# Attention over three merged key blocks: the products of blocks 1 to 3 of a group issued as one run on TensorE

## What is computed

```python
qkv = x @ Wqkv + bqkv
att = softmax(where(causal, q @ k.T * scale, -inf))     # 512 x 512 for each head
x = layernorm(x + (att @ v) @ Wout + bout)
h = silu(lin(x, w1)) * lin(x, w2)                        # 1024 hidden channels
h = gelu(lin(h, h1))
h = gelu(lin(h, h2))
x = layernorm(x + lin(h, w3))                            # lin: einsum with a weight, times a scale
```

## Time and profile before

| | us |
|---|---|
| median of 3 timed runs (2322.57 to 2328.25) | 2323.64 |
| profiled execution, its own time | 2323.13 |
| its span in the profile | 2321.4 |
| TensorE busy in it | 2208.8 (95%) |
| VectorE, ScalarE, GpSimd busy | 1278.9, 1293.6, 488.1 |
| TensorE products for `pO` (L973) | 2048 records in 209 unbroken runs: 162 of 8 and 47 of 16 |

### The profile page before, as it was taken

How to read it: one execution, slowest core, us unless ns; L and a number is a source line. 1 busy time by engine, 2 the same in 40 slices (tenths; PEclk the granted TensorE clock), 3 DMA queues, 4 the chain that set the end, 5 groups by cost and what they waited for, 6 DMA issues and landing times.

```text
span 2321.4 us, 52007 instructions
## 1 busy us (share of the span) xinstructions
PE 2208.8 (95%) x16294; PEld 1871.2 (81%) x16294; DVE 1278.9 (55%) x3961; ACT 1293.6 (56%) x2769; POOL 488.1 (21%) x896
## 2 busy tenths in 40 slices
PE   4758999999999999999999999999999999999998
PEld 2336888888888888888888888888888888888898
DVE  4564565555556556555655556565555656555433
ACT  1334566565656656565665656656565565656543
POOL 1121222122222212212221222212122221222211
PEclk7779999999999999999999999999999999999999
DMA  8642223232232323223232232323223232312000
GB/s 288 209 142 63 66 59 74 55 76 60 63 71 59 75 55 71 65 61 71 61 75 55 67 69 61 70 61 75 55 61 75 59 69 64 75 42 50 23 6 10
DMA packets 96838, 166.18 MB, mean 72 GB/s; under 512 B 21568, under 2 KB 40768, under 8 KB 96576
## 3 DMA queue, kind: packets, MB, share of 16 engines
q1 hardware_dynamic: 88736, 139.02, 25.9%
q10 hardware_dynamic: 7840, 23.86, 3.0%
HBM read 93.08 MB, written 71.83 MB: 71 GB/s over the span
## 4 chain that ended last, share of the span: by engine, by line
PE 77%; DMA 4%; issue 3%; SPq 3%; ACT 2%; DVE 2%; POOL 0%; ACTq 0%; DVEq 0%; POOLq 0%
PE ring L1055 38%; PE ring L1041 8%; PE pM L951 6%; PE pO L973 6%; PE pS L939 6%; PE ring L1068 5%; PE ring L985 4%; PE ring L1021 2%; DMA dn<-den_d 2%; DMA qk_d<-c 2%; PE ring L1005 1%; SPq L504 1%; DVE full_g L805 1%; PE ring L959 1%; ACT L698 1%
## 5 line engine op out<-in xcount | busy, mean ns | idle before, releaser
L766 DVE CUSTOM_DVE_ANT_0 pM<-pM,mask 128x512 f32<-128x512 f32 (+3 forms) x1024 | 493.4, 507 | 318.7 <-PE pM L951 262.5
L1055 PE MATMUL ring<-Xhi,H 128*128 128x256 f32 x2048 | 515.4, 291 | 6.6 <-ACT full_h L711 5.0
L1055 PE MATMUL ring<-Yhi,H 128*128 128x256 f32 x2048 | 507.4, 285 | 0.0
L1055 PE MATMUL ring<-Ylo,H 128*128 128x256 f32 x2048 | 502.8, 283 | 0.0
L1055 PE MATMUL ring<-Xlo,H 128*128 128x256 f32 x2048 | 499.3, 282 | 0.0
L1055 PEld LDWEIGHTS ring<-Xhi,H 128*128 128x128 f32 x2048 | 391.1, 191 | 18.7 <-ACT full_h L711 11.7
L1055 PEld LDWEIGHTS ring<-Ylo,H 128*128 128x128 f32 x2048 | 390.9, 191 | 3.2
L1055 PEld LDWEIGHTS ring<-Xlo,H 128*128 128x128 f32 x2048 | 392.1, 191 | 1.1
L1055 PEld LDWEIGHTS ring<-Yhi,H 128*128 128x128 f32 x2048 | 390.2, 191 | 2.6
L951 PE MATMUL pM<-Ks,Qs 128*128 128x512 f32 x992 | 297.4, 358 | 48.4 <-DMA Ks<-qk_d 31.4
L710 ACT ACTIVATE Yhi<-ring,cols 128x256 fp32r<-128x256 f32 x256 | 120.8, 472 | 285.8 <-PE ring L1055 251.2
(11 more groups left out here) (102 smaller groups left out, 3336.8 us busy)
## 6 DMA issues: line engine op xcount, KB each, us to landing
qk_d<-c SPq DMA_DIRECT2D x124, 256.0 KB, 3.4
Qs<-qk_d SPq DMA_DIRECT2D x124, 192.0 KB, 4.4
Ks<-qk_d SPq DMA_DIRECT2D x124, 192.0 KB, 4.9
qk_d<-c SPq DMA_DIRECT2D x124, 128.0 KB, 3.1
xTs<-in_xT SPq DMA_DIRECT2D x16, 512.0 KB, 4.4
raw<-in_h ACTq DMA_DIRECT2D x8, 1024.0 KB, 24.5
xz<-in_x SPq DMA_DIRECT2D x16, 512.0 KB, 6.5
Oc<-Osb SPq DMA_DIRECT2D x256, 32.0 KB
```

The lines of the kernel that those rows point to most:

```text
L766: nc.vector.tensor_tensor_reduce(pM[:, h % 2, 0:n], pM[:, h % 2, 0:n], mask[:, T - n:T], 1.0, NEG, ALU.add, ALU.max, mx[:, t, h:h + 1]).th ...
L1055: mm = nc.tensor.matmul(to, w, x_part, start=(k == 0 and m == 0), stop=(k == KB - 1 and m == 1))
```

## The change

`pv` has only two steps for a group now: `pv:0:g:0` (block 0) and `pv:0:g:1` (blocks 1, 2 and 3 in one unbroken run, 24 records), and `pv_done` counts 2 for a group instead of 4. The merged step stands where `pv:0:g:3` or `pv:0:g:2` stood. The products of block 1 move back to it; in group 1 those of block 2 also do. Blocks 2 and 3 are stored in `probs_a`, in the room of block 0 (columns 0 to 255 and 256 to 383 of each head's 512), block 1 alone in `probs_b`. All other steps keep their order among themselves. `HEAD_ORDER` and `FIRST_ORDER` are changed alike.

```diff
-h2:-2:1:1:0 exp:0:0:10 max:0:1:2:0 h2:-2:1:1:1 max:0:1:2:1 pv:0:0:1 ln1_stats:-1 max:0:1:2:2 max:0:1:2:3
+h2:-2:1:1:0 exp:0:0:10 max:0:1:2:0 h2:-2:1:1:1 max:0:1:2:1 ln1_stats:-1 max:0:1:2:2 max:0:1:2:3
-table:0:Gelu:1 h2:-2:1:2:0 h_act:-2:h2:1:0 o_out:0:0 stack:0:2 h2:-2:1:2:1 pv:0:0:2 pv:0:0:3 h_act:-2:h2:1:1
+table:0:Gelu:1 h2:-2:1:2:0 h_act:-2:h2:1:0 o_out:0:0 stack:0:2 h2:-2:1:2:1 pv:0:0:1 h_act:-2:h2:1:1
...
-gu:-1:0:3 ffn_hi:-1:0:2 ffn_hi:-1:0:3 gu:-1:0:4 max:0:2:2:1 gu:-1:0:5 ffn_hi:-1:0:4 pv:0:1:1 exp:0:1:10
-gu:-1:0:6 ffn_hi:-1:0:5 gu:-1:0:7 ffn_hi:-1:0:6 pv:0:1:2 max:0:2:2:2 max:0:2:2:3 ffn_hi:-1:0:7
-table:0:Gelu:3 pv:0:1:3 o_out:0:1 stack:0:3 h1:-1:0:0:0 h1:-1:0:0:1 h_act:-1:h1:0:0 max:0:2:1:0 max:0:2:1:1
+gu:-1:0:3 ffn_hi:-1:0:2 ffn_hi:-1:0:3 gu:-1:0:4 max:0:2:2:1 gu:-1:0:5 ffn_hi:-1:0:4 exp:0:1:10
+gu:-1:0:6 ffn_hi:-1:0:5 gu:-1:0:7 ffn_hi:-1:0:6 max:0:2:2:2 max:0:2:2:3 ffn_hi:-1:0:7
+table:0:Gelu:3 pv:0:1:1 o_out:0:1 stack:0:3 h1:-1:0:0:0 h1:-1:0:0:1 h_act:-1:h1:0:0 max:0:2:1:0 max:0:2:1:1
...
-exp:0:2:8 max:0:3:2:1 exp:0:2:9 max:0:3:2:2 pv:0:2:1 max:0:3:2:3 exp:0:2:10 h2:-1:0:2:0 h2:-1:0:2:1
-h_act:-1:h2:0:0 pv:0:2:2
-table:0:Gelu:5 pv:0:2:3 o_out:0:2 stack:1:0 h_act:-1:h2:0:1 h_rest:-1:h2:0:0 h_act:-1:h2:0:2 max:0:3:1:0
+exp:0:2:8 max:0:3:2:1 exp:0:2:9 max:0:3:2:2 max:0:3:2:3 exp:0:2:10 h2:-1:0:2:0 h2:-1:0:2:1
+h_act:-1:h2:0:0 
+table:0:Gelu:5 pv:0:2:1 o_out:0:2 stack:1:0 h_act:-1:h2:0:1 h_rest:-1:h2:0:0 h_act:-1:h2:0:2 max:0:3:1:0
...
-ffn_hi:-1:1:5 gu:-1:1:7 ffn_hi:-1:1:6 pv:0:3:1 exp:0:3:10 max:1:0:3:2 max:1:0:3:3 ffn_hi:-1:1:7 v:1:0 pv:0:3:2
-table:0:Gelu:7 pv:0:3:3 o_out:0:3 stack:1:1 max:1:0:2:0 max:1:0:2:1 h1:-1:1:0:0 h1:-1:1:0:1 h_act:-1:h1:1:0
+ffn_hi:-1:1:5 gu:-1:1:7 ffn_hi:-1:1:6 exp:0:3:10 max:1:0:3:2 max:1:0:3:3 ffn_hi:-1:1:7 v:1:0 
+table:0:Gelu:7 pv:0:3:1 o_out:0:3 stack:1:1 max:1:0:2:0 max:1:0:2:1 h1:-1:1:0:0 h1:-1:1:0:1 h_act:-1:h1:1:0
...
+        probs = (probs_a, probs_b, probs_a[:, :, :, 0:T // 2], probs_a[:, :, :, T // 2:T // 2 + P])
...
-            return (probs_b if kt % 2 else probs_a)[:, p]
+            return probs[kt][:, p]
...
-                        need(act, pv_done, b * (NG * TB) + g * TB + kt - 1)
+                        need(act, pv_done, (b * NG + g) * 2 + (kt > 1))
...
-                            dst = probs_b[:, :, :, 0:n].rearrange("k p s n -> k (p s) n")
+                            dst = probs[kt].rearrange("k p s n -> k (p s) n")
...
-                        need(act, pv_done, b * (NG * TB))
+                        need(act, pv_done, b * (NG * 2))
...
-                        act.wait_ge(pv_done, b * (NG * TB) + (g + 1) * TB)
+                        act.wait_ge(pv_done, (b * NG + g + 1) * 2)
...
-                        g, kt = a
-                        n = e_cols(kt)
-                        if kt == 0:
+                        g, rest = a
+                        if not rest:
                             if g == 0:
                                 pe.wait_ge(v_copied, (b + 1) * TB)
                             need(pe, o_out, b * NG + g)
-                        pe.wait_ge(mask_done, b * (NG * TB * PAIRS) + e_of(g, kt, PAIRS - 1) + 1)
-                        for p in range(PAIRS):
...
+                        for kt in range(1, TB) if rest else (0,):
+                            n = e_cols(kt)
+                            pe.wait_ge(mask_done, b * (NG * TB * PAIRS) + e_of(g, kt, PAIRS - 1) + 1)
+                            for p in range(PAIRS):
...
```

More of the change, by code:

```diff
@@ L120 @@
 load_x:0 stack:0:3 neg_max:0:1 pv:0:0:0 max:0:2:2:0 exp:0:0:6 max:0:2:2:1 exp:0:0:7 max:0:2:2:2 exp:0:0:8
-max:0:2:2:3 exp:0:0:9 max:0:2:1:0 exp:0:0:10 pv:0:0:1 max:0:2:1:1 max:0:2:1:2 exp:0:1:0 o_out:0:0 max:0:2:1:3
-pv:0:0:2 pv:0:0:3 max:0:2:0:0 max:0:2:0:1 exp:0:1:1 exp:0:1:2 max:0:2:0:2 max:0:2:0:3 weights:0:0 weights:0:1
+max:0:2:2:3 exp:0:0:9 max:0:2:1:0 exp:0:0:10 max:0:2:1:1 max:0:2:1:2 exp:0:1:0 o_out:0:0 max:0:2:1:3
+pv:0:0:1 max:0:2:0:0 max:0:2:0:1 exp:0:1:1 exp:0:1:2 max:0:2:0:2 max:0:2:0:3 weights:0:0 weights:0:1
 exp:0:1:3 neg_split:0:2 max:0:3:3:0 max:0:3:3:1 neg_max:0:2 exp:0:1:4 max:0:3:3:2 max:0:3:3:3 exp:0:1:5
 exp:0:1:6 max:0:3:2:0 max:0:3:2:1 qk:1:0 max:0:3:2:2 exp:0:1:7 max:0:3:2:3 weights:0:2 weights:0:3 pv:0:1:0
-exp:0:1:8 max:0:3:1:0 exp:0:1:9 pv:0:1:1 max:0:3:1:1 exp:0:1:10 pv:0:1:2 max:0:3:1:2 max:0:3:1:3 exp:0:2:0
-exp:0:2:1 max:0:3:0:0 pv:0:1:3 max:0:3:0:1 max:0:3:0:2 exp:0:2:2 max:0:3:0:3 stack:1:0 neg_split:0:3 o_out:0:1
+exp:0:1:8 max:0:3:1:0 exp:0:1:9 max:0:3:1:1 exp:0:1:10 pv:0:1:1 max:0:3:1:2 max:0:3:1:3 exp:0:2:0
+exp:0:2:1 max:0:3:0:0 max:0:3:0:1 max:0:3:0:2 exp:0:2:2 max:0:3:0:3 stack:1:0 neg_split:0:3 o_out:0:1
 qk:1:1 weights:0:4 neg_max:0:3 max:1:0:3:0 exp:0:2:3 max:1:0:3:1 max:1:0:3:2 exp:0:2:4 max:1:0:3:3 max:1:0:2:0
 exp:0:2:5 exp:0:2:6 max:1:0:2:1 pv:0:2:0 max:1:0:2:2 exp:0:2:7 max:1:0:2:3 weights:0:5 exp:0:2:8 max:1:0:1:0
-exp:0:2:9 max:1:0:1:1 pv:0:2:1 exp:0:2:10 max:1:0:1:2 max:1:0:1:3 pv:0:2:2 exp:0:3:0 max:1:0:0:0 max:1:0:0:1
-exp:0:3:1 max:1:0:0:2 max:1:0:0:3 weights:0:6 exp:0:3:2 neg_split:1:0 exp:0:3:3 pv:0:2:3 o_out:0:2 exp:0:3:4
+exp:0:2:9 max:1:0:1:1 exp:0:2:10 max:1:0:1:2 max:1:0:1:3 pv:0:2:1 exp:0:3:0 max:1:0:0:0 max:1:0:0:1
+exp:0:3:1 max:1:0:0:2 max:1:0:0:3 weights:0:6 exp:0:3:2 neg_split:1:0 exp:0:3:3 o_out:0:2 exp:0:3:4
 exp:0:3:5 weights:0:7 exp:0:3:6 neg_max:1:0 pv:0:3:0 stack:1:1 exp:0:3:7 exp:0:3:8 qk:1:2 exp:0:3:9
-weight_test:0:0 exp:0:3:10 pv:0:3:1 o_out:0:3 den:0 v:1:0 v:1:1 pv:0:3:2 pv:0:3:3 v:1:2 weight_test:0:1
+weight_test:0:0 exp:0:3:10 o_out:0:3 den:0 v:1:0 v:1:1 pv:0:3:1 v:1:2 weight_test:0:1
 weight_test:0:2 weight_test:0:3 weight_test:0:4 rec_save:0 rec_load:0 weight_test:0:5 weight_test:0:6
@@ L140 @@
 exp:0:0:4 exp:0:0:5 exp:0:0:6 exp:0:0:7 pv:0:0:0 exp:0:0:8 max:0:1:3:2 max:0:1:3:3 exp:0:0:9 max:0:1:2:0
-exp:0:0:10 max:0:1:2:1 pv:0:0:1 max:0:1:2:2 max:0:1:2:3 y:-1:0:1 y:-1:1:0 max:0:1:1:0 pv:0:0:2 pv:0:0:3
-max:0:1:1:1 o_out:0:0 stack:0:2 y:-1:1:1 max:0:1:1:2 max:0:1:1:3 max:0:1:0:0 max:0:1:0:1 max:0:1:0:2
+exp:0:0:10 max:0:1:2:1 max:0:1:2:2 max:0:1:2:3 y:-1:0:1 y:-1:1:0 max:0:1:1:0 pv:0:0:1 max:0:1:1:1 o_out:0:0 stack:0:2 y:-1:1:1 max:0:1:1:2 max:0:1:1:3 max:0:1:0:0 max:0:1:0:1 max:0:1:0:2
 max:0:1:0:3 neg_split:0:1 ln1_stats:-1 neg_max:0:1 table:0:Exp:2 qk:0:3 load_xT:1 ln1:-1 exp:0:1:0 exp:0:1:1
@@ L968, in iteration @@
                             need(pe, o_out, b * NG + g)
-                        pe.wait_ge(mask_done, b * (NG * TB * PAIRS) + e_of(g, kt, PAIRS - 1) + 1)
-                        for p in range(PAIRS):
[L971 to L975, removed]
+                        for kt in range(1, TB) if rest else (0,):
+                            n = e_cols(kt)
+                            pe.wait_ge(mask_done, b * (NG * TB * PAIRS) + e_of(g, kt, PAIRS - 1) + 1)
+                            for p in range(PAIRS):
+                                for s in range(2):
+                                    j = 2 * p + s
+                                    mm = nc.tensor.matmul(pO[32 * j:32 * j + VW, kt * P:T], Vo[:, kt, G * g + j],
+                                                          probs_of(kt, p)[:, s, 0:n],
+                                                          start=(kt == 0), stop=(kt == TB - 1))
                         mm.then_inc(pv_done, 1)
```

## The result

The changed kernel took 2327.2 us (median of 20 runs, 2323.41 to 2332.44) against 2323.51 before (20 runs, 2321.14 to 2328.25). The ratio is 1.0015, with a 95% interval of 1.0009 to 1.0022. The interval doesn't reach 1, so the change is slower, by 2 to 5 us; that is less than the 0.3% (7 us) from which the forecast would have called it a change. 2327.4 was forecast. The profiled execution has a span of 2325.7 us, 4.3 more than before.

A forecast was written before the change was run, and what follows sets the result against it. TensorE's own queue was taken to bound the steady state. Terms of 9.1 + 0.6 - 1.7 - 4.5 for the groups and +0.8 for the start sum to +4.3 us, so 2327.4 us; range 2317 to 2335.

The forecast's parts named there:

- The border of a run: Around narrow products on TensorE: entry 0.09, exit 0.11, stretch of the next full-width product 0.10, together 0.30 us.
- The merged run: Block 1 takes 0.66 us, block 2 0.45, block 3 with its exit 0.33; no full border between blocks 1 and 2.
- the fourth rival: The change doesn't do what it says: the 0.11 us might belong to every block's end; plus 8 us, chance 0.03.
- the second rival: Group 3's masks come too late, and a seam between blocks 1 and 2 costs up to 0.30; 2332 us, chance 0.22.
- Group 0 loses 0.65: `max` 2:3 waits for 2:1's reduction, which eats the saved switch; block 1's 0.66 us remain; loses 0.65 us.
- Group 2 loses 0.04: `max` 2:3 waits for 2:1 and starts 0.62 us earlier, against 0.66 more in the run; loses 0.04 us.
- Group 1 gains 0.11: Two runs go, but `gu` 7 waits for the bank of `gu` 4; gains 0.11 us, not 0.60.
- Group 3 gains 0.30: Block 3's masks are just in time for the merged run, so nothing waits; gains 0.30 us.
- The sum for the steady state: Group terms over the items: 14 x 0.65 + 15 x 0.04 - 15 x 0.11 - 15 x 0.30 us.
- The first rival: The switches are saved and nothing takes their place: 81 x 0.30 = 24 us faster, 2299; chance 0.08.
- ScalarE's waits in front of `exp`: ScalarE's waits for `pO` in front of `probs_a` or `probs_b` are gone; ScalarE isn't the bound, so nothing gained.
- +0.8 us for item 0 and the beginning of item 1: Merging puts ScalarE's next `exp` behind block 3's mask while TensorE has slack; +0.8 us, from -2 to +3.

The follow-up runs named there:

- e2_split: Kernel before, with group 0's blocks 2 and 3 parted by half of an `h2` block; one run of 2329.97 us beside 2324.83.
- e5_spread0: Changed kernel with group 0's `max` 2:3 moved behind the first half of the `h2` block; ran once, 2311.27 us beside 2324.83.
- e3_g0: Kernel before with the storage and item 0 of e1_buffers, only group 0's three blocks merged; one run of 2334.56 us beside 2324.83.
- e1_buffers: Kernel before with the new storage and its waits, products in old places except in item 0; one run of 2320.28 us beside 2324.83.
- e7_best: Kernel before with new storage, changed item 0, merged runs except block 1 in group 1, maxima moved in groups 0 and 2; 2303.68 us, ratio 0.9914.
- e6_first: Changed kernel, but the beginning of item 1 keeps group 0's three runs in the places of before; 2326.96 us, ratio 1.001.
- e8_spread0_timed: Same kernel as e5_spread0, timed beside the others; 2315.41 us (median of 6) against 2325.12, ratio 0.9954.

## Why the prediction was right, point by point

- **The border of a run, 0.30 us.** Right as a whole, by e2_split (0.30) and e5_spread0 (0.29), and in its three parts by e2_split.
- **The merged run.** 0.66 + 0.45 + 0.33 = 1.44 was forecast, 1.42 measured (1029.02 to 1030.44). Block 1 takes 0.65 in it (0.66 was forecast), so the seam between blocks 1 and 2 adds nothing. That rules out the fourth rival, and the seam's part of the second.
- **Group 0 loses 0.65.** 0.68. The spacings of 1.21 and 1.49 us came out to the hundredth. e3_g0 has nearly the whole loss (0.63) by this merge alone, and e5_spread0 takes it away with one moved step, so the cause is shown: TensorE's third product waits for the first one's reduction. The wait was to grow by some 8 us in all and grew by 11.4: 14 x 0.68 = 9.5 is this wait, and the rest are waits of changing length elsewhere.
- **Group 2 loses 0.04.** It gained 0.04 by the table, but e1_buffers gives 0.06 of storage; against that, 0.02 lost. The 0.80 us from `max` 2:2 to `exp` 10 are those of the forecast (0.52 + 0.28), so the short wait stretches the product too.
- **Group 1 gains 0.11.** 0.17, or 0.13 against e1_buffers. `gu` 7 started 2.63 us behind `gu` 5 (1024.88 to 1027.51), as worked out (1018.84 to 1021.47 there).
- **Group 3 gains 0.30.** 0.34 by medians, 0.26 against e1_buffers, and 0.22 by plain means. The masks were in time, with 0.04 us to spare in item 7; the second rival didn't come, but was as near as said. That the pattern of starts is the same in every item within 0.05 us isn't so here, as group 3's stretch varies by 0.5 us already before.
- **The sum for the steady state** was 14 x 0.65 + 15 x (0.04 - 0.11 - 0.30) = 3.5 us, or 0.65 - 0.37 = 0.28 for an item with all four groups. Measured: 0.25 by the plain mean, 0.13 by medians. Against e1_buffers, which has the storage already, it is 0.32 by medians. So the order costs about what was forecast, and the storage, for which the sum had nothing, gives back some 0.2.
- **The first rival** (all 81 borders are saved, 2299) didn't come. Yet the gain was there to have: with the waits moved out of the way e7_best came to 2303.7, part of it from the older stall in group 2.
- **ScalarE's waits in front of `exp`** went, as forecast (41.0 to 0 us before `probs_b`), but 52.4 us of waits came before `o_out` instead.
- **+0.8 us for item 0 and the beginning of item 1** is the weakest term, and was 3 us too small for this execution: item 1 began 0.4 us later (162.96 to 163.37) and took 3.5 us more (139.9 to 143.4 us), most of it with the granted clock, as under e6_first. Two other things made up for it. Items 2 to 14 took only 1.8 us more, as the kernel before had a pause of 1.4 us in item 13 that the other lacks. And what follows the start of item 15 was 1.5 us shorter (248.4 to 246.9), where the chance is on the side of before: the other eight profiles, also those with item 15 nearly as before, have 245.6 to 247.3. So that the two spans differ by just the 4.3 us that were forecast is luck. The medians of 20 runs differ by 3.7 us (2 to 5), which fits the forecast without being a fine test of it; the test of the terms is in the stretches.

## What to carry to other kernels

A product that is moved out of a chain of short steps takes its cover with it: before merging, ask for each product that will now come sooner what it waits for, and add that to what the merge saves. With two buffers in turn, the third of three short products in a row needs the first one's consumer. Here that one ended 1.15 us behind the product's start, and two products had covered only 0.36; other work of TensorE between the second and the third took the wait away. What a change of shape costs is the difference of starts at its border (here 0.30 us), and that times the number of borders is an upper bound for what merging gives by itself, to be had only when the waits are moved as well. And a product that is moved back to make room (`gu` 7 in e7_best) starts its own chain later, which can come back as a wait further on.

## What was not expected

- Behind a product that was waited for, the next one starts 0.10 us later than otherwise, as behind a run's end: 0.28 instead of 0.18 us in group 0 (1129.88 to 1130.16 after, 1122.62 to 1122.80 in e5_spread0), and the same in group 2.
- In some executions single items have a pause that the others lack: 32.07 instead of 30.7 us for group 2 of item 13 before, 40.2 instead of 38.4 us for group 1 of item 5 in e2_split (which has three more, in group 2 of items 5, 9 and 13), and others in e1_buffers and e8_spread0_timed. Medians keep them out. The order of the products there is the same as in the neighbours. The trace shows what is waited for: VectorE's `full_g` for the first of the eight `gu` also needs the transfers into `qk_d` (`qk_saved`). In item 13 before, and in item 11, which has no pause:

```profile
1892.92 0.48 DVE L805 SCALAR_TENSOR_TENSOR full_g<-ring,cols,th 128x256 f32<-128x256 f32 x1 [2.04 <-DMA qk_d<-c]
```

```profile
1619.31 0.48 DVE L805 SCALAR_TENSOR_TENSOR full_g<-ring,cols,th 128x256 f32<-128x256 f32 x1 [0.69 <-DMA qk_d<-c]
```

  The last of these transfers landed 4.50 us after its issue in item 13 (at 1892.90) and 3.16 after it in item 11 (at 1619.29); in e2_split it is 5.05 in item 5 and 3.26 in item 7. From `full_g` the delay goes on to ScalarE and TensorE. Why these single transfers took longer stays open.
- Odd and even items, which are two copies of the same steps in the loop, differ by 0.17 us in group 0 before (28.18 and 28.01). The cause was not looked for.
